# Layer norm, landmark attention and a ternary gated FFN: from one program block per batch to one block for all, with the attention mask applied after the exponential

## What is computed

```python
xn = layernorm(x)
# landmarks: 33% of the tokens with the highest score, widened by 2 on both sides
score = 0.7 * norm(xn) - 0.3 * dot(xn, mean) / (norm(xn) * norm(mean) + 1e-6)
mask = (j <= i) & ((i - j < 128) | landmark[j])      # query i, key j
q = xn @ Wq            # 16 heads of 16
k, v = xn @ Wk, xn @ Wv  # 8 heads of 16, each for two query heads
s = softmax(q @ k.T / 4 + where(mask, 0, -10000)) @ v @ Wo
h = gelu(xn @ ternary(w1).T + b1)     # 1024 wide
g = silu(h @ ternary(w2).T + b2)
out = x + s * g
```

## Time and profile before

| | us |
|---|---|
| median of 3 runs (735.44 to 738.63) | 738.3 |
| the profiled execution | 737.96 |
| its span, first to last instruction | 736.3 |
| PE busy | 628.7 (85%) |
| ACT busy | 475.7 (65%) |
| DVE busy | 375.4 (51%) |
| POOL busy | 74.7 (10%) |
| mean granted clock of PE | 0.935 of full speed |

### The profile page before, as it was taken

One profiled execution on the slowest core, in us unless ns is written; L12 is line 12 of the kernel. 1 busy time (PEld: TensorE's weight loads), 2 busy tenths in 40 slices (PEclk: granted clock), 3 DMA queues, 4 the chain that ended last, 5 costly groups with the idle time before them and its releaser, 6 DMA issues. The chain is left out here.

```text
span 736.3 us, 11753 instructions
## 1 busy us (share of the span) xinstructions
PE 628.7 (85%) x4336; PEld 351.7 (48%) x4336; DVE 375.4 (51%) x1002; ACT 475.7 (65%) x723; POOL 74.7 (10%) x92
## 2 busy tenths in 40 slices
PE   0537809999999989999999679999999899799982
PEld 0524604664455546654554536654554556334532
DVE  7968961665827434767454615648364521410101
ACT  1112417677877766697768556697768666888680
POOL 4000020020010201020100301110100210201001
PEclk9968957999999979999999869999999899899997
DMA  7000699000145659001190756001082691030101
GB/s 214 0 0 1 83 89 153 9 8 20 47 62 77 73 116 144 16 8 31 35 124 21 83 143 102 11 8 58 16 115 37 80 137 42 7 90 8 52 10 49
DMA packets 46833, 43.84 MB, mean 60 GB/s; under 512 B 6065, under 2 KB 41394, under 8 KB 46770
## 3 DMA queue, kind: packets, MB, share of 16 engines
...
## 5 line engine op out<-in xcount | busy, mean ns | idle before, releaser
L812 ACT ACTIVATE probs<-sc_ps,shift 128x512 f32<-128x512 f32 (+1 forms) x288 | 175.8, 617 | 102.0 <-PE sc_ps L725 101.3
L718 PE MATMUL sc_ps<-q_stack,k_stack 99*128 99x512 bf16 (+3 forms) x768 | 198.5, 344 | 33.3 <-PEq L189 14.7
L815 ACT ACTIVATE probs<-sc_ps,key_bias 128x1024 f32<-128x1024 f32 (+3 forms) x256 | 204.9, 818 | 16.5 <-PE sc_ps L718 15.8
L738 PE MATMUL att_ps<-probs,v_sb 128*32 128x512 f32 (+3 forms) x1536 | 167.4, 508 | 0.0
L718 PEld LDWEIGHTS sc_ps<-q_stack,k_stack 99*128 99x128 bf16 x768 | 50.2, 99 | 182.9 <-issue 70.8
L725 PE MATMUL sc_ps<-near_mask,mask_ident 128*128 128x256 bf16 (+1 forms) x576 | 105.1, 266 | 0.0
L850 POOL TENSOR_TENSOR h_lo<-hid,h_hi 128x512 fp32r<-128x512 f32 x32 | 43.2, 1350 | 342.3 <-DVE h_hi L882 342.3
L725 PEld LDWEIGHTS sc_ps<-near_mask,mask_ident 128*128 128x128 bf16 x576 | 56.4, 103 | 37.5 <-issue 7.1
L665 PE MATMUL aux_ps<-w2T,h_hi 128*128 128x256 f32 x256 | 70.1, 307 | 0.0
L665 PE MATMUL aux_ps<-w2T,h_lo 128*128 128x256 f32 x256 | 63.2, 279 | 0.0
L773 ACT ACTIVATE hid<-aux_ps,b_sb 128x512 f32<-128x512 f32 x64 | 42.9, 687 | 22.8 <-PE aux_ps L655 13.8
...
## 6 DMA issues: line engine op xcount, KB each, us to landing
...
xn<-in_L_attn_hidden_states SPq DMA_DIRECT2D x4, 1024.0 KB, 8.2
attT<-att_raw SPq DMA_DIRECT2D x128, 32.0 KB
...
probs<-in_L_ffn_w SPq DMA_DIRECT2D x2, 1024.0 KB, 7.8
...
```

The source lines that it names most:

```text
L718: last = pe.matmul(sc_ps[:, 2 * u + hh, lo:CH], k_stack[0:KROWS + SHIFT_ROWS, h // REP, kb * P:(kb + 1) * P], q_stack[0:KROWS + SHIFT_ROWS ...
L738: last = pe.matmul(att_ps[32 * q:32 * q + 32, n % 2, lo:CH], v_sb[:, kb, j * VW:j * VW + 32], probs[:, i % 3, q, lo:CH], start=(kb == 0), ...
L812: last = act.activation(probs[:, i % 3, us, lo:near], sc_ps[:, us, lo:near], ACT.Exp, bias=shift[:, 0:1], scale=HD ** -0.5)
L815: last = act.activation(probs[:, i % 3, us, near:CH], sc_ps[:, us, near:CH], ACT.Exp, bias=key_bias[:, kb:kb + 1], scale=HD ** -0.5)
```

## The change

The kernel becomes three parts: a set-up, a `general_path` (the old program, taken if the scores' bound is too large) and a `fast_path`, chosen by one branch. What follows is the fast path.

- One block for all batches: steps s = 0 to 191 with no barrier between batches, 24 preparing steps ahead. Jobs of a batch reach into its neighbours' steps: the last `out_proj` of a batch runs at steps 57 and 58 (9 and 10 of the next), `ffn_down` of chunk 0 at 10 to 17, `v_proj` at 42, and the two sets of `ffn_up` with their table changes at 18 and 44.
- The mask is applied to the exp's results. L718's matmul has no second one behind it; ACT does one exp of each half; POOL zeroes the triangle of the diagonal block in `probs` (`causal`, an affine select of 128 x 4 x 128, 128 of them); DVE multiplies the next block by a near mask (`local`, 128 x 4 x 128, 112 of them). Later columns use `v_far`, the values multiplied by the landmark of their key, so that `values` has two sets of four matmuls where both kinds are present. `values` waits for both engines. `commit` makes the near masks and `v_far` at a batch's step 0. There are four `probs` buffers, not three.
- The query stack holds three slots of one group each, and `fill_q` loads a group with 6 DMAs of 64 KB when the group three back is through; `fill_k` loads two key heads' rows with 6 DMAs.
- The sum over tokens for the mean is made on POOL (7 adds of 128 x 256) and takes one matmul, not eight; norms come from the variance, so a pass over xn goes.
- The set-up has tiles of its own, and no longer clears `q_stack` and `k_stack`.

```diff
-        FFN_DOWN_AT = (6, 7, 8, 9, 10, 11, 12, 13)
...
-                jobs += [(C1 - 0.5, "ffn_up", 1, f, f) for f in range(FT)]
-                jobs += [(C1 + at, "out_proj", t, n_prev + t) for t, at in enumerate((11, 13, 15, 16))]
-                jobs += [(C1 + 18 + 2 * t + half, "ffn_down", TC + t, half) for t in range(TC) for half in range(2)]
...
-                    jobs += [(NSTEP + 3, "v_proj", i) for i in range(2)]
-                    jobs += [(NSTEP + (0 if f < 2 else LAG), "ffn_up", 0, f, FT + f) for f in range(FT)]
...
-                                last = pe.matmul(sc_ps[:, 2 * u + hh, lo:near], mask_ident[:, :], near_mask[:, first:end:kb + 1, :],
-                                                 start=False, stop=True)
...
-                            if near > lo:
-                                last = act.activation(probs[:, i % 3, us, lo:near], sc_ps[:, us, lo:near], ACT.Exp,
-                                                      bias=shift[:, 0:1], scale=HD ** -0.5)
-                            if near < CH:
-                                last = act.activation(probs[:, i % 3, us, near:CH], sc_ps[:, us, near:CH], ACT.Exp,
-                                                      bias=key_bias[:, kb:kb + 1], scale=HD ** -0.5)
-                            last.then_inc(exp_done, 1)
...
-        turn(None, False, True, False, None)
-        turn(0, True, True, False, x[1])
-        with nc.Fori(1, B - 1) as b:
-            turn(b, True, True, True, x[b + 1])
-        turn(B - 1, True, False, True, None)
...
+                        jobs += [(p + 16, "mean_row", b)]
+                        jobs += [(p + at, "transpose", b, n % KD, n // KD) for n, at in enumerate((19, 19, 20, 21))]
+                        jobs += [(p + 22 + c, "k_proj", b, c) for c in range(NC)]
+                        jobs += [(p + at, "q_proj", b, n % QT, n // QT) for n, at in enumerate((24, 26, 29, 31))]
+                        jobs += [(p + 30, "score_row", b, i) for i in range(2)]
+                        jobs += [(p + 41, "dilate", b)]
+                        jobs += [(p + 42, "v_proj", b, i) for i in range(2)]
+                        jobs += [(p + 43.5, "ffn_up", b, 0, f) for f in range(FT)]
...
+                    jobs += [(o + 10 + i, "ffn_down", b, i // 2, i % 2) for i in range(2 * TC)]
+                    jobs += [(o + 17.5, "ffn_up", b, 1, f) for f in range(FT)]
+                    jobs += [(o + 27 + t, "out_proj", b, t) for t in range(TC)]
+                    jobs += [(o + 34 + i, "ffn_down", b, TC + i // 2, i % 2) for i in range(2 * TC)]
+                    jobs += [(o + (57 + t // 2), "out_proj", b, TC + t) for t in range(TC)]
...
+                        def fill_q(n):
+
+                            b, c, g = n // NG, n % NG // GROUPS, n % GROUPS
+                            m = g // QT
+                            if n >= QSLOTS:
+                                sp.wait_ge(sc_done, 2 * (GEND[n - QSLOTS] + 1))
+                            sp.wait_ge(q_split, QT * NC * b + QT * c + m + 1)
+                            for i in range(NPART):
+                                src = q_parts[half_rows(g), m, QPART[i], c * CH:(c + 1) * CH]
+                                sp.dma_start(q_stack[i * HD:(i + 1) * HD, n % QSLOTS, :, :], src).then_inc(q_in[n % QSLOTS], 16)
+
+                        def fill_k(b, g):
+                            if b:
+                                sp.wait_ge(sc_done, 2 * (GEND[(b - 1) * NG + GROUPS + g] + 1))
+                            sp.wait_ge(k_split, NC * (b + 1))
+                            for i in range(NPART):
+                                src = k_parts[g * 2 * HD:(g + 1) * 2 * HD, KPART[i], :]
...
+                            for n in range(B * NG):
+                                if GEND[n] + 1 == s:
+                                    if n + QSLOTS < B * NG:
+                                        fill_q(n + QSLOTS)
+                                    if n % NG >= GROUPS and b < B and n // NG + 1 < B:
+                                        fill_k(n // NG + 1, n % GROUPS)
+                            if 0 <= s < TOTAL and i == 0 and b + 1 < B:
+                                sp.wait_ge(aux_done, first_job[("transpose", b, KD - 1, NC - 1)] + 1)
+                                sp.wait_ge(dots_done, T * (b + 1))
+                                sp.wait_ge(xsum_done, b + 1)
+                                sp.dma_start(xn[:, :, :], x[b + 1].rearrange("(t p) d -> p t d", p=P)).then_inc(x_next_in, 16)
...
+                            if s % NSTEP == 0:
+                                pe.wait_ge(far_done, b + 1)
+                            pe.wait_ge(exp_done, 2 * (s + 1))
+                            if has_tri(s % NSTEP):
+                                pe.wait_ge(tri_done, TRIS[s])
+                            if has_local(s % NSTEP):
+                                pe.wait_ge(local_done, LOCALS[s])
+                            lo, end = spans(s % NSTEP)
+                            ends = [(v_sb[:, b % 2], lo, end), (v_far, end, CH)]
+                            for w, first, stop in ends:
+                                if first == stop:
+                                    continue
+                                for q in range(NQ):
+                                    j = (g * NQ + q) // REP
+                                    last = pe.matmul(att_ps[32 * q:32 * q + 32, n % 2, first:stop], w[:, kb, j * VW:j * VW + 32],
+                                                     probs[:, s % NPROB, q, first:stop], start=(kb == 0 and first == lo),
+                                                     stop=(kb == TC * (c + 1) - 1), skip_group_check=True)
+                            last.then_inc(pv_done, 1)
...
+                            act.activation(probs[:, s % NPROB, us, lo:CH], sc_ps[:, us, lo:CH], ACT.Exp,
+                                           bias=shift[:, 0:1], scale=HD ** -0.5).then_inc(exp_done, 1)
...
+                        def token_sum(b):
+                            if b:
+                                pool.wait_ge(aux_done, first_job[("mean_row", b - 1)] + 1)
+                            for t in range(1, T):
+                                pool.wait_ge(xn_done, T * b + t + 1)
+                                ins = pool.tensor_tensor(xsum[:, :], xn[:, 0, :] if t == 1 else xsum[:, :], xn[:, t, :], ALU.add)
+                                if t < T - 1:
+                                    lk(ins)
+                                else:
+                                    ins.then_inc(xsum_done, 1)
...
+                        def causal(s):
+                            c, _, kb = STEPS[s % NSTEP]
+                            own_q = slice((kb - TC * c) * P, (kb - TC * c + 1) * P)
+                            block_probs = probs[:, s % NPROB, :, own_q]
+                            pool.wait_ge(exp_done, 2 * (s + 1))
+                            pool.affine_select(out=block_probs, in_=block_probs, compare_op=ALU.is_ge, fill=0.0, base=0,
+                                               pattern=[[0, NQ], [1, P]], channel_multiplier=-1).then_inc(tri_done, 1)
...
+                        def commit(b):
+                            dve.wait_ge(v_done, 2 * (b + 1))
+                            if b:
+                                dve.wait_ge(pv_done, b * NSTEP - 2)
+                                dve.wait_ge(local_done, LOCALS[b * NSTEP - 1])
+                            for t in range(T - 1):
+                                dve.tensor_scalar(near[:, t, :], before[:, :], landmark[:, t:t + 1], None, ALU.max)
+                            dve.tensor_tensor(v_far[:, :, :], v_sb[:, b % 2], landmark[:, :].unsqueeze(2).to_broadcast([P, T, VP]),
+                                              ALU.mult).then_inc(far_done, 1)
+                            dve.wait_ge(far_done, b + 1)
+
+                        def local(s):
+                            c, _, kb = STEPS[s % NSTEP]
+                            nxt = slice((kb + 1 - TC * c) * P, (kb + 2 - TC * c) * P)
+                            block_probs = probs[:, s % NPROB, :, nxt]
+                            dve.wait_ge(exp_done, 2 * (s + 1))
+                            dve.tensor_tensor(block_probs, block_probs, near[:, kb, :].unsqueeze(1).to_broadcast([P, NQ, P]),
+                                              ALU.mult).then_inc(local_done, 1)
```

2104 lines of the change are left out of this document (1324 added, 780 removed).

## The result

The changed kernel takes 787.1 us (783.5 to 791.1, four runs), the kernel before 737.3 (735.4 to 738.6): a ratio of 1.068, interval [1.062, 1.074]. The prediction was 722 with a range to 747. The profiled execution took 788.1, its span is 786.2.

What follows compares the result with a forecast made beforehand. PE was taken to bound chunk 1, chains through DVE and DMA the time before the first values. 738.0 - 21.1 + 1.8 - 6.4 + 10 - 1 + 0.4 = 721.7 us, range 694 to 747.

Steps and rivals of the forecast that it cites:

- The start, -21.1: Set-up to first values: threshold -8.3, mean and norms -2.3, landmarks to first values -11.5, branch +1; together -21.1 us.
- For the branch to distant code I add +1: In the start: the branch to the new path's distant code costs 1 us.
- Chunk 1: Chunk 1 with both gelu sets: 112.0 us against 115.4, with sum and clock terms +0.6 in each of three turns.
- Steps without a job are bound by the chain below or by ACT: +3.7: Chunk 1 steps without a job: bound by exp, mask, values or by ACT, adding 3.7 us.
- The chain: Exp, mask, values: DVE's multiply 0.69 and POOL's select 0.65 serially, values free 1.5 us after their step's second exp.
- Rival (c): Slower: POOL's causal select takes 1.35 us instead of 0.65, chain decides in about 36 steps, total 747; chance 0.19.
- `token_sum`, +2.3: Steps 14 and 15: POOL's sum, 5.5 us, queued ahead of the causal selects, delays PE's values by 2.3 us.
- Clock after the gelus, +1.7: Behind the first gelus: PE idles, goes on at 0.50 of its clock, and ACT waits 1.7 us more.
- The cold start behind the second set: Behind the second gelus: PE's cold start takes the place of that behind the barrier, no extra time.
- Chunk 0 of batches 1 to 3: DMA queueing makes chunk 0 about 46 us in batches 1 and 2, +10 together; batch 3 takes 39, -1.
- rival a: Chunk 0: wait for den does not bite, mask and select overlap; some 38 us, total 701; chance 0.24.
- Batch 3 loads no x and no keys: Chunk 0 of batch 3: without those loads it takes 39 us, -1.

Runs made afterwards that it cites:

- e1: Changed kernel without either masking of the exp's results and without the values' waits for them: 735.5 us.
- e4: Changed kernel with POOL's sum over the tokens, and the mean's matmul, two steps later: 767.7 us.
- e3: Changed kernel with values three steps behind the scores instead of two, group copies one step later: 768.3 us.
- e15: Changed kernel with thirteen useless matmuls on PE behind the first scores after each set of gelus: 771.4 us.
- e9: Changed kernel with the causal mask as a matmul on the scores and POOL's sum two steps later: 767.5 us.
- e18: Against the best complete variant (six edits to the changed kernel, 750.8 us): reciprocals not spread, division by the sums of weights left out: 728.7 us.

## Why the prediction was wrong

**The start, -21.1, measured -6.8 with chunk 0 of batch 0.** The first values came at 111.2 us, where 95 was forecast and 116.2 stood before. The threshold was ready at 16.86 (17.0 forecast), and commit took 3.9 us from the landmarks to the first values (3.0). What failed is "For the branch to distant code I add +1" and what followed from it: DVE stood 5.2 us in issue at the first instruction of the new path and POOL 7.5 us at its third, the sum's first addition, 3.5 of them after the last token was normalised. The same stands are in e1 to e4; that the branch is their cause, no run shows. The mean came at 53.5, not at 46.6 (DVE's copy of it at 56.17 before, less 8.3 and 2.3, and 1 more). From there the landmarks took 53.7 us where it had been 45.5: four of the ranks now stand in DVE's queue behind all splits of the gelus. In the executions with PE at half clock from 79 to 90 us, of which the one shown is one, DVE idles for the first gelu as well and the first exp comes at 98; with full clock there (e3, e15) at 93.

**Chunk 1, "Steps without a job are bound by the chain below or by ACT: +3.7".** This is the step that failed and that decided: chunk 1 was 14.4 us a turn too low. The chain was priced as 1.5 us behind the exp, with DVE and POOL free when it ends. The multiplies take 0.69 us and the selects 0.64 as forecast (below), but in DVE's queue a multiply waits behind transposes that wait for PE, splits, products and reciprocals. The masks together cost 12.9 us a turn in chunk 1 (e1), where this term and that of POOL's sum had 3.7 + 2.3. Rival (c) was right in sign and wrong in mechanism: it wanted selects of 1.35 us; they took 0.64, and their own length cost no more than the matmuls that can replace them (e9).

**`token_sum`, +2.3.** Right place, wrong size: 6.3 (e4).

**Clock after the gelus, +1.7.** Right mechanism and too small: 2.2 to 2.6 behind each set, and there are seven. The cold start behind the second set is there as forecast (granted 0.62 over the first 8.9 us, 1.00 in e15), but it was priced at nothing, in the barrier's place.

These sizes overlap, since the clock has a part in the masks' price. Taken as if they did not, the masks are 12.9 - 6.0 = 6.9 us over their terms and the clock 2.7 to 3.5 over its own, so some 4 to 5 of the 14.4 us a turn stay unattributed.

**Chunk 0 of batches 1 to 3.** 46 us for batches 1 and 2 was right (46.3), and so were the stand at the reciprocals and its place. But that this stand makes the 46 us, with 38 left where it does not bite (rival a), was not: without the masks chunk 0 still takes 44.6 and 46.2, since PE then waits for attT (e1), and it comes to 41 only in e18, which leaves the spreading out. For batch 3, 39 was wrong by 6.7: "Batch 3 loads no x and no keys" missed that its own last keys are refilled by the same six DMAs at the start of it, and that the spreading holds `out_proj` there too. The prediction had the chain's pieces, and did not see that the barrier that was removed had hidden it.

**The sum of the terms** came out where a wait was priced by what is queued ahead of it (chunk 0) and failed where an operation was priced by its own duration (chunk 1).
